# L1 attention's small products moved onto halves of TensorE's rows: 51 rows each, masks first

## The chip, the cores and the metric

One core of one Trainium2 chip runs the whole program in one launch. The metric is device time in microseconds (us), median of the runs shown. The program is a chain of eight layers (four attention-like, four feed-forward) over a residual stream of 2048 tokens by 512 channels; the change touches the third of them, called L1 attention.

## What is computed

The part of the reference that matters here, shortened:

```python
x = x + layernorm(L1_attn(layernorm(x), Wqkv, Wo))

def L1_attn(h, Wqkv, Wo):             # h: 2 batches x 1024 tokens x 512
    qkv = h @ Wqkv                    # 32 query heads of 16, one key and one value head of 16
    q, k, v = split(qkv)
    scores = einsum("bqhd,bkd->bhqk", q, k) * 16 ** -0.5
    scores = scores + alibi           # slope of the head x (key position - query position)
    scores = where(causal, scores, -1e30)
    return (softmax(scores) @ v).reshape(...) @ Wo
```

All heads share one key and one value. The head dimension is only 16, so that a plain score product has 16 rows to contract.

## The kernel before

**Contraction.** Queries and keys are held as pairs of float16 numbers (high part and rest). The rows of `a2_qs` and `a2_ks` stack the parts: four blocks of D2 = 16 rows hold qh, qh, ql, ql against kh, kl, kh, kl (QR = 64), two rows add the ALiBi term (QR to QR+2), and one more row (QR+2) carries minus the row maximum. A maximum product contracts 66 rows, a score product 67. `a2_qs` is [67 rows used, 32 heads, 1024 queries] per batch, `a2_ks[b]` [67 rows, 1024 keys].

**Loops.** Queries go in 16 tiles of 128 (SEQ2: eight of batch 0 in order, then batch 1's as 0, 3, 1, 4, 2, 5, 6, 7). Query tile t attends to t+1 key blocks. For each tile two things are made:

- its *maxima* (`max_unit`): [128 queries x up to 512 keys] for as many heads as fit a PSUM bank, one product a head (L1259), and over the last 128 keys of the diagonal block one identity product with the mask (L1262) for each head; VectorE then reduces the bank to one maximum a head (L1425). Three banks (0 to 2) form this ring.
- its *scores* (`score_unit`): [128 keys x 4 heads x 128 queries] (L1272), on the diagonal block a mask product over all 512 columns (L1275); ScalarE takes the exponential (L1381) out of banks 3 to 5. After four of them `value_units` (L1282) multiplies by the values: four float32 products, which the trace shows as eight, on four column strips of 32 into bank 6.

**Order.** `plan2`, `tails2` and `steps2` write one list, STEPS2, that all engines walk. While tile p's scores are made, tile p+1's maxima are slipped between them, and also the work on the tile before (`heads0` to `lo`: transposes L1323, L1329 and L1342, projection L332 to L334, layer norm). TensorE takes them strictly in that order. A maximum waits until VectorE has emptied its bank (`a2_md`), a score until ScalarE has emptied its own (`a2_e`). A `row` step turns a tile's maxima (L1300) and a DMA (L1197) puts them into row QR+2.

**DMAs.** SyncE copies the key parts (L1189, 4 DMAs a batch) and, for each half batch of 512 queries, the query parts (`q_rows`, L1205): 8 heads x 4 blocks = 32 DMAs. The first maximum of tiles 0 and 4 of a batch waits on `a2_dma` for them.

```python
            for rep, src in enumerate((a2_qh, a2_qh, a2_ql, a2_ql)):
                sp.dma_start(a2_qs[rep * D2:(rep + 1) * D2, h:H2:8, gg * GW:(gg + 1) * GW],
                             src[h * D2:(h + 1) * D2]).then_inc(a2_dma, 16)
```

## Time and profile before

| | us |
|---|---|
| median of 3 runs | 4417.35 |
| lowest, highest | 4415.72, 4435.38 |
| profiled execution, its time | 4429.2 |
| its span in the trace | 4427.4 |
| L1 attention in the trace, first copy of weights to last value product | 660 to 1471 |
| first to last score product | 743 to 1470 |

| engine, whole span | busy us | share |
|---|---|---|
| TensorE products | 3811.0 | 86% |
| VectorE | 2844.1 | 64% |
| ScalarE | 2291.2 | 52% |
| GpSimd | 1786.5 | 40% |

TensorE's busy time counts a product to the end of its pipeline, so products overlap in it; what it can deliver is read from the distance of the starts. "PEclk" is the granted clock as a share of 2.4 GHz; half of it is 1.2 GHz.

### The profile page before, as it was taken

The page shows a single profiled execution, that of the slowest core. Times are in us where ns is not written, and L with a number is a line of the kernel's source. Part 1 is how long each engine was busy: PE and PEld are TensorE (multiplying, and loading weights), DVE is VectorE, ACT ScalarE, POOL GpSimd, SP SyncE. Part 2 cuts the span into 40 slices and gives each one's busy share as a digit, 9 for nine tenths or more (in the row PEclk, how much of TensorE's full clock was granted, in tenths as well). Part 3 has the DMA queues.
Part 4 walks back from the last instruction along what each step waited for, and adds up shares of the span by engine and source line. Part 5 has one row for each costly group of instructions (what it writes and reads, how often), then busy time and mean ns, then how long its engine had stood idle before and what let it go on. Part 6 is the DMA issues. An engine that isn't in the chain of part 4 may idle for free.

```text
span 4427.4 us, 62775 instructions
## 1 busy us (share of the span) xinstructions
PE 3811.0 (86%) x21328; PEld 1913.2 (43%) x21328; DVE 2844.1 (64%) x4571; ACT 2291.2 (52%) x3974; POOL 1786.5 (40%) x1454
## 2 busy tenths in 40 slices
PE   6799995998899648999999999999999966756699
PEld 3344442333333224555555555555555533432344
DVE  6522223674576357888888898888889866566322
ACT  5422222455456436667666676766676644442222
POOL 5400000000000006778787877777787864420000
PEclk9799997889889879999999999999999988897899
DMA  3100001101100010000000000000000010005100
GB/s 108 44 1 0 0 7 35 20 1 21 20 1 1 10 56 12 19 17 7 29 1 24 12 24 13 24 13 13 23 7 23 1 60 1 26 1 137 41 10 19
DMA packets 67429, 97.53 MB, mean 22 GB/s; under 512 B 14081, under 2 KB 39689, under 8 KB 67098
## 3 DMA queue, kind: packets, MB, share of 16 engines
q1 hardware_dynamic: 67100, 93.47, 7.8%
q8 instruction: 166, 2.72, 0.3%
q14 instruction: 163, 1.34, 0.1%
HBM read 77.77 MB, written 6.88 MB: 19 GB/s over the span
## 4 chain that ended last, share of the span: by engine, by line
PE 63%; DVE 15%; issue 8%; ACT 6%; POOL 3%; SPq 3%; DMA 2%; DVEq 0%; POOLq 0%; ACTq 0%
PE psum L332 14%; PE psum L333 13%; PE psum L334 13%; PE psum L1282 3%; PE psum L1259 3%; DVE arena L1425 2%; PE psum L1272 2%; PE psum L2255 2%; PE psum L2243 2%; PE psum L2251 2%; PE psum L2212 2%; SPq L1205 1%; ACT xn L218 1%; PE psum L2234 1%; DVE x L1940 1%
## 5 line engine op out<-in xcount | busy, mean ns | idle before, releaser
L332 PE MATMUL psum<-xt_hi,arena 128*128 128x512 f16 (+1 forms) x2272 | 878.4, 387 | 81.3 <-DVE arena L538 24.3
L333 PE MATMUL psum<-xt_lo,arena 128*128 128x512 f16 (+1 forms) x2272 | 876.3, 386 | 0.0
L334 PE MATMUL psum<-xt_hi,arena 128*128 128x512 f16 (+1 forms) x2272 | 874.7, 385 | 0.0
L2038 POOL TENSOR_TENSOR arena<-arena 128x1024 f16<-128x1024 f16 x256 | 515.3, 2032 | 193.2 <-DVE arena L1850 148.9
L1215 POOL TENSOR_TENSOR rs<-sd,epsc 128x1 f32<-128x1 f32 x16 | 8.8, 548 | 1204.8 <-DVE sd L1469 1204.8
L1425 DVE TENSOR_REDUCE arena<-psum 128x1 f32<-128x512 f32 (+3 forms) x608 | 367.4, 654 | 188.6 <-PE psum L1262 114.7
L332 PE MATMUL psum<-arena 128*128 128x512 f16 (+1 forms) x1152 | 417.7, 367 | 82.1 <-DVE arena L2810 36.3
L1381 ACT ACTIVATE arena<-psum 128x512 f32<-128x512 f32 x576 | 324.4, 598 | 274.9 <-PE psum L1272 181.0
L333 PE MATMUL psum<-arena 128*128 128x512 f16 (+1 forms) x1152 | 417.0, 366 | 0.0
L334 PE MATMUL psum<-arena 128*128 128x512 f16 (+1 forms) x1152 | 416.7, 366 | 0.0
L332 PEld LDWEIGHTS psum<-xt_hi,arena 128*128 128x128 f16 x2272 | 225.5, 99 | 334.9 <-DVE arena L538 27.3
L334 PEld LDWEIGHTS psum<-xt_hi,arena 128*128 128x128 f16 x2272 | 225.6, 99 | 278.9 <-issue 19.0
L333 PEld LDWEIGHTS psum<-xt_lo,arena 128*128 128x128 f16 x2272 | 225.5, 99 | 238.5 <-issue 15.0
L2043 POOL TENSOR_TENSOR arena<-arena 128x512 f16<-128x512 f16 x256 | 316.3, 1254 | 4.2 <-PE psum L2223 4.2
L538 DVE SCALAR_TENSOR_TENSOR arena<-psum,arena 128x512 f32<-128x512 f32 x100 | 69.1, 691 | 355.1 <-PE psum L334 351.5
L1259 PE MATMUL psum<-arena 66*128 66x512 f16 (+3 forms) x768 | 247.3, 362 | 53.9 <-DMA arena<-arena 33.0
L1940 DVE SCALAR_TENSOR_TENSOR x<-arena,x 128x512 f32<-128x512 f32 x288 | 283.5, 985 | 15.4 <-ACT x L1757 8.6
L1940 DVE SCALAR_TENSOR_TENSOR arena<-arena 128x512 f32<-128x512 f32 x288 | 275.3, 956 | 6.8
L2065 POOL TENSOR_TENSOR arena<-arena 128x256 f32<-128x256 f32 x128 | 148.7, 1162 | 250.4 <-ACT arena L1809 250.4
L508 ACT ACTIVATE arena<-psum 128x512 f32<-128x512 f32 x100 | 59.5, 595 | 345.1 <-PE psum L334 345.1
L1272 PE MATMUL psum<-arena 67*128 67x512 f16 x576 | 227.4, 410 | 5.6 <-ACT arena L1381 3.2
L332 PEld LDWEIGHTS psum<-arena 128*128 128x128 f16 x1152 | 124.0, 108 | 195.3 <-DVE arena L2810 36.8
(310 smaller groups left out, 7771.7 us busy)
## 6 DMA issues: line engine op xcount, KB each, us to landing
arena<-m_wi SPq DMA_DIRECT2D x64, 320.0 KB, 2.9
arena<-arena SPq DMA_DIRECT2D x128, 64.0 KB, 2.5
arena<-m_wo SPq DMA_DIRECT2D x32, 256.0 KB, 2.6
arena<-out SPq DMA_DIRECT2D x6, 768.0 KB, 5.9
x<-L_attn_x SPq DMA_DIRECT2D x4, 1024.0 KB, 8.7
out<-x SPq DMA_DIRECT2D x4, 1024.0 KB, 4.3
arena<-gate_wT SPq DMA_DIRECT2D x16, 224.0 KB, 2.5
arena<-up_wT SPq DMA_DIRECT2D x16, 224.0 KB, 2.5
```

The lines of the kernel that those rows point to most:

```text
L332: nc.tensor.matmul(out, lh, rh, start=start, stop=False)
L333: nc.tensor.matmul(out, lh, rl, start=False, stop=False)
L334: return nc.tensor.matmul(out, ll, rh, start=False, stop=stop)
L1259: last = nc.tensor.matmul(out[:, a * w:(a + 1) * w], q, a2_ks[b][0:QR + 2, c:c + w], start=True, stop=not diag)
L1272: last = nc.tensor.matmul(out, a2_ks[b][0:QR + 3, k * P:(k + 1) * P], a2_qs[0:QR + 3, h4 * 4:h4 * 4 + 4, t * P:(t + 1) * P], start=True, s ...
L1282: last = nc.tensor.matmul(psum[j * VW:(j + 1) * VW, 6, :], a2_v[b][:, g % (t + 1), :], a2_ps[(group2[p] + g) % 3][:, j, :], start=False, s ...
L1381: nc.scalar.activation(a2_ps[group % 3][:, u[0] % 4, :], psum[:, 3 + e % 3, :], ACT.Exp).then_inc(a2_e, 1)
L1425: nc.vector.tensor_reduce(a2_mx[:, q % 2, c // 512, h0:h0 + heads], bank[:, 0:heads * w].rearrange("p (h c) -> p h c", h=heads), AXX, ALU. ...
L1940: v = nc.vector.scalar_tensor_tensor(out=out, in0=m4_hb[:, i, j:j + GW], scalar=m4_cp[:, i * KC + j:i * KC + j + 1], in1=out, op0=ALU.mult ...
L2038: nc.gpsimd.tensor_tensor(m4_ar[:, q], heads[q].broadcast_to([P, HG, P]), m4_le.unsqueeze(1).broadcast_to([P, HG, P]), ALU.mult).then_inc( ...
L2043: nc.gpsimd.tensor_tensor(m4_ab[:, q].rearrange("p (h c) -> p h c", c=PS), heads[q].broadcast_to([P, HG, PS]), m4_on[:, 0:PS].unsqueeze(1) ...
L2065: nc.gpsimd.tensor_tensor(m4_sq[:, 0:2, :], m4_sq[:, 0:2, :], m4_sq[:, 2:4, :], ALU.add).then_inc(m4_qs, 1)
```

## The change

The lowest block of products, ql against kl, is dropped: QR = 48, so that a maximum contracts 50 rows and a score 51. The 32 heads are split into two sets of 16, heads with (h div 4) even on partitions 0 to 50, the others on 64 to 114 (`row_group`); the keys stand on both. Products thereby name an array tile of 64 rows x 128 columns at row 0 or 64, where the old ones, and still the masks, named 128 x 128.

`max_units` lists the units of the two sets in turn, and `paired2` gives each maximum of STEPS2 a unit of the set that the last score or maximum before it did not use. The mask of a maximum is now one identity product for all heads of the unit, ahead of their products, which accumulate onto it; the mask of a score still follows it. There are 608 maximum units before and after (352 with a mask), and 576 scores (128 with a mask); mask products of the maxima go from 512 to 352, over the same columns.

```diff
-        QR = 4 * D2
-        a2_qs = carve(0, [H2, TPB * P], F16)
+        QR = 3 * D2
+        HALF = 64
+        a2_qs = carve(0, [H2 // 2, TPB * P], F16)
-        QDMA = 4 + 4 * 8 * 2
+        KDMA, HDMA = 3 * 2, 3 * 8
+        QDMA = KDMA + HDMA * 2
...
-                    units += [(h, 512 // w, first, w) for h in range(0, H2, 512 // w)]
+                    units += [(g * (H2 // 2) + h, 512 // w, first, w) for h in range(0, H2 // 2, 512 // w)
+                              for g in range(2)]
...
+        def row_group(half, first, n):
+            return slice(half * HALF + first, half * HALF + first + n)
...
+        def paired2():
+            left, unit, half = {}, {}, 1
+            for what, p, *u in STEPS2:
+                if what == "score":
+                    half = u[0] % 2
+                elif what == "ring" and RING2[p][0] == "max":
+                    q, n = RING2[p][1:]
+                    rest = left.setdefault(q, list(max_units(SEQ2[q][1])))
+                    other = [m for m in rest if m[2] == rest[0][2] and m[0] // (H2 // 2) != half]
+                    unit[q, n] = other[0] if other else rest[0]
+                    rest.remove(unit[q, n])
+                    half = unit[q, n][0] // (H2 // 2)
+            return unit
...
-                for rep, src in enumerate((a2_qh, a2_qh, a2_ql, a2_ql)):
-                    sp.dma_start(a2_qs[rep * D2:(rep + 1) * D2, h:H2:8, gg * GW:(gg + 1) * GW],
+                for rep, src in enumerate((a2_qh, a2_qh, a2_ql)):
+                    sp.dma_start(a2_qs[row_group(h // 4, rep * D2, D2), h % 4:H2 // 2:4, gg * GW:(gg + 1) * GW],
                                  src[h * D2:(h + 1) * D2]).then_inc(a2_dma, 16)
...
+                h0, heads, c, w = UNIT2[p, u]
+                rows = row_group(h0 // (H2 // 2), 0, QR + 2)
+                diag = c + w == (t + 1) * P
+                if diag:
+                    nc.tensor.matmul(out.rearrange("p (a w) -> p a w", w=512 // heads)[:, :, w - P:w], a2_id,
+                                     a2_mqk.unsqueeze(1).broadcast_to([P, heads, P]), start=True, stop=False,
+                                     skip_group_check=True)
                 for a in range(heads):
...
+                    last = nc.tensor.matmul(out[:, a * w:(a + 1) * w], a2_qs[rows, h0 % (H2 // 2) + a, t * P:(t + 1) * P],
+                                            a2_ks[b][rows, c:c + w], start=not diag, stop=True, skip_group_check=True)
...
+                rows = row_group(h4 % 2, 0, QR + 3)
+                last = nc.tensor.matmul(out, a2_ks[b][rows, k * P:(k + 1) * P],
+                                        a2_qs[rows, h4 // 2 * 4:h4 // 2 * 4 + 4, t * P:(t + 1) * P], start=True,
+                                        stop=(k < t))
```

**TensorE, the maxima of a tile with 384 keys between another's scores.** Before: L1259 is a maximum's product, L1262 its mask, L1272 a score, L1282 the values.

```order
L1259 MATMUL psum<-arena 128x384
L1262 MATMUL psum<-arena 128x128
L1259 MATMUL psum<-arena 128x384
L1262 MATMUL psum<-arena 128x128
L1272 MATMUL psum<-arena 128x512
L1282 MATMUL psum<-arena 32x512 x4
```

After: L1283 is the mask, L1287 the maximum's product, L1298 the score, L1309 the values.

```order
L1283 MATMUL psum<-arena 128x128
L1287 MATMUL psum<-arena 128x384
L1283 MATMUL psum<-arena 128x128
L1287 MATMUL psum<-arena 128x384
L1298 MATMUL psum<-arena 128x512
L1309 MATMUL psum<-arena 32x512 x4
```

The mask stands ahead of its product; each mask names the whole array, its neighbours now half of it.

**TensorE, a unit of four heads with 128 keys, between scores.** Before, a mask behind each head:

```order
L1259 MATMUL psum<-arena 128x128
L1262 MATMUL psum<-arena 128x128
L1259 MATMUL psum<-arena 128x128
L1262 MATMUL psum<-arena 128x128
L1259 MATMUL psum<-arena 128x128
L1262 MATMUL psum<-arena 128x128
L1259 MATMUL psum<-arena 128x128
L1262 MATMUL psum<-arena 128x128
L1272 MATMUL psum<-arena 128x512
```

After, one mask ahead of all four:

```order
L1298 MATMUL psum<-arena 128x512
L1283 MATMUL psum<-arena 128x512
L1287 MATMUL psum<-arena 128x128 x4
L1298 MATMUL psum<-arena 128x512
L1283 MATMUL psum<-arena 128x512
L1287 MATMUL psum<-arena 128x128 x4
```

Four mask products became one of four times the columns.

**SyncE, the first half of batch 0** (key parts, query parts, rows of maxima). Before:

```order
L1180 DMA arena<-mask_qk 128x128
L1181 DMA arena<-mask_kq 128x128
L1189 DMA arena<-arena 16x1024 [waits a2_md]
L1189 DMA arena<-arena 16x1024 x3
L1205 DMA arena<-arena 16x4x512 [waits a2_md]
L1205 DMA arena<-arena 16x4x512 x31
L1197 DMA arena<-arena 1x32x128 [waits a2_e] x3
```

After:

```order
L1203 DMA arena<-mask_qk 128x128
L1204 DMA arena<-mask_kq 128x128
L1213 DMA arena<-arena 16x1024 [waits a2_md]
L1213 DMA arena<-arena 16x1024 x5
L1229 DMA arena<-arena 16x4x512 [waits a2_md]
L1229 DMA arena<-arena 16x4x512 x23
L1221 DMA arena<-arena 2x16x128 [waits a2_e] x3
```

Six key DMAs stand where four were, and 24 query DMAs, of the same size each, where 32 were. Three more small copies (of the ALiBi rows) stand ahead of these.

## Rows read from the trace of the kernel before

**Rows 1.** Engines by stretch: busy us and count of each, PEclk, DMA share, GB/s.

```profile
core 0: us, PE busy (x) PEld busy (x) DVE busy (x) ACT busy (x) POOL busy (x), PEclk, DMA share, GB/s
934.00:1040.00 106.00, 98.39 (x587) 35.68 (x585) 80.87 (x153) 65.54 (x119) 2.19 (x4) 1.00 0.00 1
1086.00:1098.00 12.00, 8.27 (x60) 5.50 (x61) 3.32 (x5) 1.79 (x3) 0.00 (x0) 0.57 0.17 26
1165.00:1190.00 25.00, 21.54 (x66) 6.66 (x67) 11.89 (x21) 7.22 (x13) 0.00 (x0) 0.52 0.08 13
743.00:1470.00 727.00, 662.81 (x3739) 251.79 (x3739) 437.04 (x834) 383.44 (x695) 16.44 (x30) 0.89 0.06 10
```

**Rows 2.** Waits, 743 to 1470: who waited for whom, us, times, longest.

```profile
PEld psum L1259 <- DVE arena L1425: 122.7, 202, 2.4
DVE arena L1425 <- PE psum L1262: 90.8, 73, 16.0
```

**Rows 3.** Groups by line and form, 934 to 1040: count, busy us, mean ns, idle before.

```profile
L1272 PE MATMUL psum<-arena 67*128 67x512 f16 x104 | 39.3, 380 | 0.0
L1259 PE MATMUL psum<-arena 66*128 66x512 f16 x88 | 32.2, 383 | 2.0 <-DVE arena L1425 2.0
L1282 PE MATMUL psum<-arena 128*32 128x512 f32 x208 | 27.7, 605 | 0.0
L1262 PE MATMUL psum<-arena 128*128 128x128 f16 x64 | 14.1, 220 | 0.0
L1272 PEld LDWEIGHTS psum<-arena 67*128 67x128 f16 x104 | 10.1, 98 | 9.8 <-ACT arena L1381 2.0
L1259 PE MATMUL psum<-arena 66*128 66x384 f16 x32 | 10.0, 329 | 1.8 <-DVE arena L1425 1.6
```

**Rows 4.** TensorE in order of time around a group of values: start, us, engine, line.

```profile
1007.83 0.38 PE L1272 MATMUL psum<-arena 67*128 67x512 f16 x1
1008.14 1.06 PE L1282 MATMUL psum<-arena 128*32 128x512 f32 x8
1009.13 0.39 PE L1259 MATMUL psum<-arena 66*128 66x512 f16 x1
1009.36 0.22 PE L1262 MATMUL psum<-arena 128*128 128x128 f16 x1
1009.42 0.38 PE L1272 MATMUL psum<-arena 67*128 67x512 f16 x1
1009.64 0.38 PE L1259 MATMUL psum<-arena 66*128 66x512 f16 x1
```

**Rows 5.** First layers: durations (min/median/max ns) of L1025, then products in order.

```profile
L1025 PE MATMUL psum<-ident,xn x128: 417/421/478, 10.1 to 187.6; 128*128 128x128 f32 x128
...
69.76 1.11 PE L1025 MATMUL psum<-ident,xn 128*128 128x128 f32 x4
70.80 1.86 PE L1052 MATMUL psum<-arena 4*128 4x448 f32 x2
```

**Rows 6.** The same view around a transpose of 32 columns.

```profile
1112.09 0.22 PE L1262 MATMUL psum<-arena 128*128 128x128 f16 x1
1112.15 0.27 PE L1300 MATMUL psum<-ident,arena 128*32 128x128 f32 x1
1112.26 0.38 PE L1272 MATMUL psum<-arena 67*128 67x512 f16 x1
```

**Rows 7.** SyncE in order of time: the copies of key and query parts.

```profile
692.64 2.52 SPq L1189 DMA_DIRECT2D arena<-arena  x4
703.13 21.33 SPq L1205 DMA_DIRECT2D arena<-arena  x32
```

**Rows 8.** TensorE in order of time: its three waits for these copies, in brackets.

```profile
726.49 0.27 PE L1259 MATMUL psum<-arena 66*128 66x128 f16 x1 [22.36 <-DMA arena<-arena]
...
1089.73 0.27 PE L1259 MATMUL psum<-arena 66*128 66x128 f16 x1 [4.82 <-DMA arena<-arena]
...
1168.46 0.58 PE L1259 MATMUL psum<-arena 66*128 66x512 f16 x1 [5.83 <-DMA arena<-arena]
```

More of the change, by code:

```diff
@@ L709, in build @@
         group2 = [first2[p] // 4 for p in range(NT)]
+        def paired2():
[11 more added lines that the diff above has]
+            return unit
+        UNIT2 = paired2()
         s3_raw = carve(0, [KT, C], F32)
@@ L1175, in sp_l1_attn @@
             sp.dma_start(a2_rwo, A["L1_attn_Wo"].rearrange("(k p) n -> p k n", p=P)).then_inc(a2_in, 16)
-            sp.dma_start(a2_qs[QR:QR + 2], A["alibi_q"]).then_inc(a2_in, 16)
-            for b in range(NB):
-                sp.dma_start(a2_ks[b][QR:QR + 3], A["alibi_k"]).then_inc(a2_in, 16)
+            for half in range(2):
+                sp.dma_start(a2_qs[row_group(half, QR, 2)], A["alibi_q"][half]).then_inc(a2_in, 16)
+                for b in range(NB):
+                    sp.dma_start(a2_ks[b][row_group(half, QR, 3)], A["alibi_k"]).then_inc(a2_in, 16)
             sp.dma_start(a2_id, A["ident16"]).then_inc(a2_in, 16)
@@ L1187, in sp_l1_attn @@
                         sp.wait_ge(a2_md, p + 3)
-                        for rep, src in enumerate((a2_kh, a2_kl, a2_kh, a2_kl)):
-                            sp.dma_start(a2_ks[piece[1]][rep * D2:(rep + 1) * D2], src[0:D2]).then_inc(a2_dma, 16)
+                        for rep, src in enumerate((a2_kh, a2_kl, a2_kh)):
+                            for half in range(2):
+                                sp.dma_start(a2_ks[piece[1]][row_group(half, rep * D2, D2)], src[0:D2]).then_inc(a2_dma, 16)
                     elif piece == ("qp", 0, 1, KT - 1):
@@ L1224, in pe_l1_attn @@
             pe.wait_ge(a2_md, 2)
-            pe.wait_ge(a2_in, 16 * 8)
+            pe.wait_ge(a2_in, 16 * 11)
             pe.wait_ge(xt_ok, NT * (s + 1))
@@ L1253, in max_unit @@
                 if u == 0 and t in (0, 4):
-                    pe.wait_ge(a2_dma, 16 * (b * QDMA + (4 + 32 if t == 0 else QDMA)))
-                h0, heads, c, w = max_units(t)[u]
-                for a in range(heads):
-                    q = a2_qs[0:QR + 2, h0 + a, t * P:(t + 1) * P]
-                    diag = c + w == (t + 1) * P
-                    last = nc.tensor.matmul(out[:, a * w:(a + 1) * w], q, a2_ks[b][0:QR + 2, c:c + w], start=True,
-                                            stop=not diag)
-                    if diag:
-                        last = nc.tensor.matmul(out[:, (a + 1) * w - P:(a + 1) * w], a2_id, a2_mqk, start=False,
-                                                stop=True)
+                    pe.wait_ge(a2_dma, 16 * (b * QDMA + (KDMA + HDMA if t == 0 else QDMA)))
+                h0, heads, c, w = UNIT2[p, u]
[5 more added lines that the diff above has]
+                                     skip_group_check=True)
+                for a in range(heads):
+                    last = nc.tensor.matmul(out[:, a * w:(a + 1) * w], a2_qs[rows, h0 % (H2 // 2) + a, t * P:(t + 1) * P],
+                                            a2_ks[b][rows, c:c + w], start=not diag, stop=True, skip_group_check=True)
                 return last
@@ L1271, in score_unit @@
                 out = psum[:, 3 + e % 3, :]
-                last = nc.tensor.matmul(out, a2_ks[b][0:QR + 3, k * P:(k + 1) * P],
-                                        a2_qs[0:QR + 3, h4 * 4:h4 * 4 + 4, t * P:(t + 1) * P], start=True, stop=(k < t))
+                rows = row_group(h4 % 2, 0, QR + 3)
+                last = nc.tensor.matmul(out, a2_ks[b][rows, k * P:(k + 1) * P],
+                                        a2_qs[rows, h4 // 2 * 4:h4 // 2 * 4 + 4, t * P:(t + 1) * P], start=True,
+                                        stop=(k < t))
                 if k == t:
@@ L1347, in act_l1_attn @@
             s = 2 - start
-            act.wait_ge(a2_in, 16 * 8)
+            act.wait_ge(a2_in, 16 * 11)
             nc.scalar.activation(a2_wh, a2_raw, ACT.Copy, scale=WS).then_inc(a2_whi, 1)
@@ L1359, in act_l1_attn @@
                         if b:
-                            act.wait_ge(a2_dma, 16 * (4 + 32))
+                            act.wait_ge(a2_dma, 16 * (KDMA + HDMA))
                         nc.scalar.activation(a2_kh[0:D2, gg * GW:(gg + 1) * GW], bank[0:D2, :], ACT.Copy,
@@ L1422, in dve_l1_attn @@
                         q, unit = piece
-                        h0, heads, c, w = max_units(SEQ2[q][1])[unit]
+                        h0, heads, c, w = UNIT2[q, unit]
                         dve.wait_ge(a2_ms, p + 1)
@@ L2944, in constants @@
     return {
-        "alibi_q": np.ascontiguousarray(np.broadcast_to(np.stack([hi, lo])[:, :, None], (2, 32, 1024))),
+        "alibi_q": np.ascontiguousarray(np.broadcast_to(
+            np.stack([hi, lo]).reshape(2, 4, 2, 4).transpose(2, 0, 1, 3).reshape(2, 2, 16, 1), (2, 2, 16, 1024))),
         "alibi_k": np.stack([pos, pos, np.ones(1024, np.float16)]),
```

4 lines of the change are left out of this document (2 added, 2 removed).

## The prediction

> **What bounds the kernel now.** First the table of stretches [rows 1]. From the first to the last score TensorE's products are in flight for 662.8 of 727 us, VectorE works 437.0 and ScalarE 383.4. Since a product counts to the end of its pipeline, I read what TensorE can deliver from the distance of its starts: two products of 512 columns start 0.22 us apart (1009.42 to 1009.64) [rows 4], a mask of 128 columns takes 0.06 (1009.36 to 1009.42). I take 0.216 for 512 columns. In 934 to 1040, all at 2.4 GHz [rows 1], the groups [rows 3] then need: 104 scores 22.5 us, 88 maxima of 512 columns 19.0, 32 of 384 columns 5.3 (0.165 each), 64 masks 3.7, 26 groups of eight value products at 0.99 (1008.14 to 1009.13) 25.7, and by count and columns about 17 for score masks, projection, keys, transposes and the way into the value products. That is 93 of 106 us, 88%; VectorE needs 80.9, 76%. The waits agree [rows 2]: TensorE's loads for a maximum wait 202 times for VectorE, 0.6 us each, and VectorE waits 73 times for a masked maximum, 1.2 us each. So TensorE is the tighter engine, and VectorE stands close behind. What TensorE gains or loses shows, but not in full; I let 0.85 of it through, between its 88% and all of it less the short waits for VectorE.
>
> **Part 1, half the rows.** Contracting 50 instead of 66 rows is worth nothing by itself: a product of 128 rows (1009.36) [rows 4] and one of 67 stream their columns at the same rate, and columns stay the same. The fewer masks (352 for 512) cover the same columns.
>
> **Part 2, changes of the array's tile.** Before, maxima, scores and masks all name 128 x 128; only the 144 groups of values (and the keys) leave it, 288 changes counted at the values. In the new order I count 554 runs of products on half the rows. Each has a way in and a way out (352 of the ways in come right behind a mask, 244 of the ways out lead to the mask of a maximum, 128 to that of a score, 192 ways touch the values); with 96 changes between values and full products these are 1204, so 916 more. What is one? Around the values [rows 4] a score starts and the values follow 0.31 us later, not 0.22: +0.09. The eight products then hold the array 0.99 us, where 2 rounds of two 512-column passes make 0.86: +0.13, with the starts of four strips in it. The next product is followed after 0.23, +0.01. Together 0.23 for two changes, 0.09 to 0.13 each; I take 0.10. Those are column strips. For rows there is one place [rows 5]: the last of four transposes starts at 69.76 + 1.11 - 0.42 = 70.45, streams four passes of 128 columns (0.21) and should be followed at 70.66; the product of 4 rows comes at 70.80, +0.14. So a change of row tile costs too, and I keep 0.09 to 0.14. Against both stands the transpose of 32 columns [rows 6]: it names another tile, and its neighbours come at 0.06 and 0.11, just their columns. That is the lower end, zero. Half of the changes have the cover of a wait at most (TensorE waits at 202 of 608 maxima); the 352 behind a mask and the 128 ahead of a score's mask have none, since nothing is waited for there.
>
> The sum of this part: 916 x 0.10 = +92 us of TensorE, from 0 to 916 x 0.14 = 128.
>
> The Trainium skill (TensorEngine Tiling (Array Packing), Key Properties) says that changing the tiling mode drains the engine, changing tiles within a mode does not. Rows 4 and 5 agree with it, rows 6 do not show it; by the page this part is the +92, by rows 6 nothing.
>
> **Part 3, opposite halves side by side.** This is the gain. The nearest row for products that share the array is the values [rows 3, 4]: eight of 605 ns, 4.8 us in all, stand in 1.06 us, on four column strips. Two row halves no row shows. If they do the same, neighbours on opposite halves cost one stream. But the planner's alternation is broken by the masks: a masked maximum is put opposite the score *before* it, the mask of the whole array stands between, and the score *after* it is on the same half: 203 runs begin with a maximum and a score of one half. Only 342 pairs of neighbours are opposite. If each product starts as soon as its own half is free, all runs together take 468,736 columns instead of 589,824: 121,088 columns, 51 us. If a following start must also wait for its own weights, 0.098 us to load [rows 3], 71,097 columns remain, 30 us. I take 40 us. The bounds are 0 and 51; a loss has no reason here.
>
> **Part 4, the copies.** 32 query copies take 21.33 us [rows 7], 0.667 each; 24 take 16.0, so 5.3 less. TensorE waits for three of the four bursts [rows 8]: 22.36, 4.82 and 5.83. The first gives 5.3, the next all of 4.8, the last 5.3: -15 us. One burst, the second in order, is not waited for and gives nothing. The two key copies more come when SyncE has nothing to do until 703.13, where it waits for the queries' low parts [rows 7]; nothing. The three more ALiBi copies stand ahead of two masks that the start of the stage needs: 0 to 3 x 0.67 = 2, I take 1. The row copies of the maxima queue behind shorter bursts; no cost. A bonus may come with it: after the two short waits the clock is granted at 0.57 and 0.52 for 12 and 25 us [rows 1]. If the waits go and the clock holds, up to half of 10 and 24 us at 1.2 GHz comes back, 17 us. I count none and keep it in the range.
>
> **The sum.** TensorE: +92 - 40 = +52, of which 0.85 shows: +44. Copies: -15 + 1 = -14. Together +30. Against the profiled execution, 4429.2 (span 4427.4), this makes 4459; that execution was 12 us above the median of 4417.35, and for the median I say 4447.
>
> **Rivals.**
>
> *The changes are hidden.* TensorE waits 122.7 us for VectorE ahead of maxima [rows 2]; if more of the drains fall into these than I let through, say the 244 ways out to a mask and a third of the others, half of the +52 remains, +26, and with the copies' -14 and a few us of clock back the time is 4424, between 4415 and 4437. For it: the load of a maximum waits on 202 of 608. Against it: 480 of the changes stand where nothing is waited for.
>
> *A change of row tile is free, as in rows 6.* This is the one on the other side. TensorE then only gains, 40 us, until VectorE's 76% becomes the bound; from 88% there is room for it, and I let 0.6 through: -24. With -14 and half of the clock's bonus, -8, the time is 4371. It decides against me when a change costs under 0.03 us: 916 x 0.03 = 27 is less than the 40 won. For it speaks one place, against it rows 4 and 5.
>
> *The clock falls.* It is granted at 0.89 over the stage [rows 1], although at 1.00 where TensorE is 88% filled. Were the empty time of the changes to bring it to 0.80, the fifth of the stage at 1.2 GHz would be two fifths: 727 x 0.18 = 131 us more at half rate, half of it lost, +65: 4512. Against it: the order has no longer waits than before.
>
> *No overlap, or no load beneath a product of the same half.* If the halves don't run side by side, 92 x 0.85 - 14 = +64: 4481. If in a run on one half the next load waits for the product, 448 pairs of neighbours on the same half pay 0.098 each [rows 3], +44, of which +37 show: 4484. The Trainium skill (TensorE: Matmul & The Clock Gate, Part 3) does say that weight loads overlap running products only where the row groups differ; by that rule it is the 4484, and the 0.22 us between starts in rows 4, each with a load of its own, does not agree with it.
>
> **How the numbers follow.** Forecast 4447 (4430 to 4470 by its own bounds): 0.44. Hidden, 4424: 0.21. Free changes, 4371: 0.17. Clock, 4512: 0.11. No overlap or no load beneath, about 4482: 0.07. About 0.5%, 22 us, is what a measurement of this kernel can tell from no change, so the borders are 4395 and 4439. Faster: 0.17 of the free changes and 0.01 of the hidden: 0.18. Within: 0.20 of the hidden and 0.13 of the forecast's lower part: 0.33. Slower: the rest, 0.49. The range from 4392 to 4500 leaves out the free changes but their upper end (0.15) and most of half of the clock case (0.05).
>
> **What the changed profile would show.** Right: from a mask to its maximum's product 0.15 us or more where 0.06 stood; a score 0.3 us behind a masked maximum's product only where a mask lies between; opposite neighbours starting 0.01 to 0.1 us apart, not 0.22; 24 query copies in 16 us, TensorE's first wait near 17 us, the short ones gone or under 1; VectorE waiting longer for maxima. The stage, 743 to 1470, should be some 44 - 10 = 34 us longer, the wait ahead of it 5 shorter, and everything after it unchanged. Wrong: masks followed after 0.06 (changes are free), opposite neighbours still 0.22 apart (no overlap), or PEclk in the stage far from 0.89.

## The result, and the profile after

The changed kernel takes 4524.5 us (median of 4 executions, 4496.6 to 4550.5) against 4416.5 for the kernel before beside it: a ratio of 1.0235, 95% interval 1.0165 to 1.0304. It is slower by about 108 us, and beyond the range. The profiled execution took 4531.8 us, its span is 4530.0 (before 4427.4), 102.6 longer.

Where does it sit? From the first to the last score took 726.1 us before and takes 825.8 now (744.7 to 1570.6). TensorE's first product of a maximum (not its mask, which now stands ahead of it) starts 4.7 earlier, and everything behind the last score is 1.5 longer (2959.4 for 2957.9). So the whole loss lies in the stage that was changed. The stretches of the profile of after (from and to, length, busy us and count of each engine, PEclk, DMA share, GB/s) say how; the first is the stage, to be held against the last line of [rows 1], the second is tile 6 of batch 0, from its first score to its last:

```profile
core 0: us, PE busy (x) PEld busy (x) DVE busy (x) ACT busy (x) POOL busy (x), PEclk, DMA share, GB/s
744.00:1570.00 826.00, 768.62 (x3611) 211.65 (x3615) 447.87 (x834) 390.43 (x696) 16.43 (x30) 0.80 0.04 7
1006.00:1090.00 84.00, 79.47 (x312) 17.05 (x311) 43.53 (x75) 36.82 (x65) 1.09 (x2) 0.67 0.00 1
```

The same tile in the kernel before:

```profile
984.00:1040.00 56.00, 52.57 (x310) 18.47 (x307) 41.59 (x75) 35.13 (x64) 1.09 (x2) 1.00 0.00 1
```

Over the stage the granted clock fell from 0.89 to 0.80. In the tile it fell from 1.00 to 0.67: 310 products on TensorE then and 312 now, 75 operations on VectorE both times, in 84 us for 56. VectorE is busy as long as before (437 to 448 us in the stage). The page's row of clocks shows the same over the whole span, a digit for each fortieth. The stage fills the eighth to the fourteenth place; they read 8898898 before, and now 9779777:

```profile
PEclk9799996977977788999999999999999997997899
```

PEclk is a mean of two levels, 1.2 GHz (0.5) and 2.4 GHz (1.0). So it can be turned into time at 1.2 GHz. From the start of the first maximum's product to the start of the last score, which I call the stage from here on, it was 159.4 of 743.0 us before and is 358.8 of 848.7 us after. (The expectations below count it from the first score on, as the fences do: 152.7 before and 335.9 after.)

The waits (who waited for whom, us, times, longest), 744 to 1570, have shifted. The lines answer to [rows 2]: VectorE waited 90.8 us for masked maxima there and 73.0 for those without a mask, together 163.8 for the 233.8 of now; ScalarE waited 181.0 for scores without a mask, now 239.6. TensorE's loads waited 122.7 for VectorE; since a mask now stands ahead of its maximum, two lines of after are their counterpart, 84.6 and 59.1.

```profile
ACT arena L1408 <- PE psum L1298: 239.6, 239, 5.3
DVE arena L1452 <- PE psum L1287: 233.8, 187, 11.1
PEld psum L1287 <- DVE arena L1452: 84.6, 133, 2.5
PEld psum L1283 <- DVE arena L1452: 59.1, 103, 1.2
```

So VectorE and ScalarE wait longer for TensorE, which is the tighter engine now as before, and more so. Its loads wait for VectorE no less than before, but TensorE itself stands empty no longer: it has no product in flight for 57.4 of 826 us (826 less 768.6), where it was 64.2 of 727. Its products in order of time at 2.4 GHz (start, us, engine, line) show both things that the change does, as [rows 4] showed the old spacing:

```profile
816.08 0.39 PE L1287 MATMUL psum<-arena 50*128 50x512 f16 x1
816.30 0.38 PE L1298 MATMUL psum<-arena 51*128 51x512 f16 x1
816.61 0.39 PE L1340 MATMUL psum<-arena 128*128 128x512 f16 x1
...
817.93 0.23 PE L1283 MATMUL psum<-arena 128*128 128x128 f16 x1
818.09 0.39 PE L1287 MATMUL psum<-arena 50*128 50x512 f16 x1
818.32 0.38 PE L1298 MATMUL psum<-arena 51*128 51x512 f16 x1
818.63 0.23 PE L1283 MATMUL psum<-arena 128*128 128x128 f16 x1
...
819.27 0.39 PE L1287 MATMUL psum<-arena 50*128 50x512 f16 x1
819.28 0.39 PE L1298 MATMUL psum<-arena 51*128 51x512 f16 x1
```

A mask (L1283) is followed after 0.16 (817.93 to 818.09) where 0.06 stood, a score by a mask after 0.31 (818.32 to 818.63) where 0.22 would stand: a change of tile costs TensorE 0.09 to 0.10, as forecast. Opposite halves start 0.01 apart (819.27, 819.28): they do run side by side. 218 of the 342 opposite neighbours start less than 0.05 apart. Two products of the same half keep 0.22 (816.08, 816.30), so a load is hidden beneath a product of its own half too. At 1.2 GHz the way in after a mask takes 0.22:

```profile
975.13 0.29 PE L1283 MATMUL psum<-arena 128*128 128x128 f16 x1
975.35 0.50 PE L1287 MATMUL psum<-arena 50*128 50x384 f16 x1
```

The copies came out as said. SyncE's queue and TensorE's first wait, the answers to [rows 7] and [rows 8]:

```profile
692.69 4.17 SPq L1213 DMA_DIRECT2D arena<-arena  x6
703.18 16.16 SPq L1229 DMA_DIRECT2D arena<-arena  x24
```

```profile
721.33 0.58 PE L1283 MATMUL psum<-arena 128*128 128x512 f16 x1 [17.15 <-DMA arena<-arena]
```

24 copies in 16.16 us, a first wait of 17.15 for 22.36, and none of the two short waits is left.

So each local event was as forecast, and the time was not. The question for the experiments is what took the clock, and how much of the loss it is.

### The profile page after: what moved, and what is told of

It is laid out like the page before. It is cut to its first block, busy times and chain, and to the rows that moved or that the text cites. A ratio compares the mean times of both kernels' runs of the same rounds, so it can differ in the third digit from the quotient of the medians.

```text
span 4530.0 us, 62430 instructions
## 1 busy us (share of the span) xinstructions
PE 3925.1 (87%) x21168; PEld 1870.2 (41%) x21168; DVE 2858.2 (63%) x4571; ACT 2296.9 (51%) x3974; POOL 1780.3 (39%) x1454
## 4 chain that ended last, share of the span: by engine, by line
PE 65%; DVE 14%; issue 8%; ACT 6%; POOL 3%; DMA 2%; SPq 2%; DVEq 0%; POOLq 0%; ACTq 0%
PE psum L332 13%; PE psum L333 13%; PE psum L334 13%; PE psum L1309 4%; PE psum L1287 4%; PE psum L1298 2%; PE psum L2282 2%; PE psum L2278 2%; DVE arena L1452 2%; PE psum L2270 2%; PE psum L2239 2%; PE psum L1283 1%; ACT xn L218 1%; PE psum L2261 1%; PE psum L1302 1%
## 5 line engine op out<-in xcount | busy, mean ns | idle before, releaser
L1452 DVE TENSOR_REDUCE arena<-psum 128x1 f32<-128x512 f32 (+3 forms) x608 | 379.4, 657 | 261.8 <-PE psum L1287 257.0
L1408 ACT ACTIVATE arena<-psum 128x512 f32<-128x512 f32 x576 | 329.9, 597 | 360.3 <-PE psum L1298 239.6
L1287 PE MATMUL psum<-arena 50*128 50x512 f16 (+3 forms) x768 | 244.9, 390 | 20.0 <-DVE arena L1452 19.8
L1298 PE MATMUL psum<-arena 51*128 51x512 f16 x576 | 231.4, 456 | 7.8 <-ACT arena L1408 5.4
```

The lines of the kernel that those rows point to most:

```text
L1287: last = nc.tensor.matmul(out[:, a * w:(a + 1) * w], a2_qs[rows, h0 % (H2 // 2) + a, t * P:(t + 1) * P], a2_ks[b][rows, c:c + w], start=no ...
L1298: last = nc.tensor.matmul(out, a2_ks[b][rows, k * P:(k + 1) * P], a2_qs[rows, h4 // 2 * 4:h4 // 2 * 4 + 4, t * P:(t + 1) * P], start=True, ...
L1408: nc.scalar.activation(a2_ps[group % 3][:, u[0] % 4, :], psum[:, 3 + e % 3, :], ACT.Exp).then_inc(a2_e, 1)
L1452: nc.vector.tensor_reduce(a2_mx[:, q % 2, c // 512, h0:h0 + heads], bank[:, 0:heads * w].rearrange("p (h c) -> p h c", h=heads), AXX, ALU. ...
```

## The experiments

All are kernels of the same program. "Changes" counts as the prediction does: how often TensorE goes from a product that names one shape of array tile to one that names another (288 before, 1204 after); the 16 transposes of 32 columns, as in [rows 6], are left out of the count. The stage is that of the profiled execution. The last column takes the price of a us at 1.2 GHz out of it; where the 0.39 comes from stands behind the twelfth kernel. The times at 1.2 GHz are each of one profiled execution. They scatter: ahead of the stage, where no edit changes TensorE's products, it is 114 us before, 190 in e5_padded and 61 in e1_rows51, and yet the first maximum starts within 7 us of the same time in all three. So a difference in that column is leaned on where the stage's length and the median time go with it, and one of a few tens of us is not leaned on by itself.

| kernel | time, us (n) | ratio to before, 95% | changes | stage, us | of it at 1.2 GHz | stage less 0.39 x that |
|---|---|---|---|---|---|---|
| before | 4416.5 (4) | | 288 | 743.0 | 159.4 | 680.8 |
| after | 4524.5 (4) | 1.0235 (1.0165 to 1.0304) | 1204 | 848.7 | 358.8 | 708.8 |
| e1_rows51 | 4759.4 (3) | 1.0774 (1.0752 to 1.0795) | 1681 | 1085.4 | 778.2 | 781.9 |
| e2_nomask | 4441.9 (9) | 1.0048 (1.0026 to 1.0069) | 288 | 760.0 | 306.2 | 640.6 |
| e3_rows51_nomask | 4563.4 (3) | 1.0326 (1.0306 to 1.0346) | 481 | 881.3 | 573.7 | 657.6 |
| e4_halves_nomask | 4440.0 (9) | 1.0050 (1.0031 to 1.0069) | 481 | 744.5 | 304.1 | 625.9 |
| e5_padded | 4398.5 (7) | 0.9956 (0.9937 to 0.9974) | 288 | 719.8 | 123.6 | 671.6 |
| e6_masks_on_halves | 4425.8 (10) | 1.0017 (1.0003 to 1.0032) | 481 | 745.2 | 180.6 | 674.8 |
| e7_mask_changes | 4607.4 (3) | 1.0435 (1.0408 to 1.0463) | 1312 | 928.8 | 477.1 | 742.7 |
| e8_rows128 | 4355.4 (5) | 0.9861 (0.9837 to 0.9885) | 288 | 683.6 | 25.0 | 673.9 |
| e9_halves_rows64 | 4458.8 (4) | 1.0081 (1.0062 to 1.0099) | 1204 | 774.0 | 168.0 | 708.5 |
| e10_masks_rows64 | 4409.7 (8) | 0.9970 (0.9958 to 0.9982) | 481 | 731.7 | 140.2 | 677.0 |
| e11_rows128_changes | 4458.0 (3) | 1.0083 (1.0059 to 1.0107) | 1312 | 783.0 | 116.7 | 737.5 |
| e12_rows128_4blocks | 4377.9 (4) | 0.9903 (0.9887 to 0.9920) | 288 | 698.9 | 43.6 | 681.9 |

Three kernels are over 2% from the before beside them in their whole interval, e1, e3 and e7; the other differences are smaller, but none of the intervals holds 1.

Two theories stood at the start: **changes** of the array's tile cost their own time and leave TensorE's array empty, and **half rows**: products that contract 51 rows for 67 are what loses the clock. A third, that the two halves side by side empty the array between them (**overlap**), was their rival. Ahead of each verdict stands one line, the stretch from the first to the last score of that kernel, with the columns of the first fence.

### Three blocks on one half, no overlap

```diff
-        QR = 4 * D2
+        QR = 3 * D2
...
-                        for rep, src in enumerate((a2_kh, a2_kl, a2_kh, a2_kl)):
+                        for rep, src in enumerate((a2_kh, a2_kl, a2_kh)):
...
-                for rep, src in enumerate((a2_qh, a2_qh, a2_ql, a2_ql)):
+                for rep, src in enumerate((a2_qh, a2_qh, a2_ql)):
```

> The kernel before with the three blocks alone: 50 and 51 rows, all heads at row 0, masks behind the products as before, 24 query copies. Nothing can run side by side; the products name the 64-row tile and the masks the whole array, so the order has 1681 changes of tile (before 288, after 1204). Theory D (each change empties the array and many of them bring the granted clock down): the changed kernel paid about 0.16 us a change, clock included, so 4417 + 1393 x 0.16 - 14 = 4626, PEclk of the stage 0.80 or less. Theory O (the clock falls because overlapped halves leave TensorE empty): clock as before, 0.89, and only the changes' own 0.1 us: 4417 + 1393 x 0.1 x 0.85 - 14 = 4521. Theory R (products on half the rows count less for the clock): clock down to 0.80 or less, time near D's.

```profile
751.00:1805.00 1054.00, 1024.55 (x3738) 272.04 (x3738) 460.21 (x834) 396.48 (x695) 16.43 (x30) 0.65 0.03 5
```

4759 us, slower than either theory allowed. With 51 rows everything on rows 0 to 63 makes 1681 changes, and 778 of 1085 us run at 1.2 GHz. The overlap can't be the cause of the lost clock: here there is none, and the loss is three times that of the change. It does not yet tell changes from half rows.

### The masks left out: of before, of e1_rows51, of after

```diff
-                    if diag:
-                        last = nc.tensor.matmul(out[:, (a + 1) * w - P:(a + 1) * w], a2_id, a2_mqk, start=False,
-                                                stop=True)
...
-                if k == t:
-                    last = nc.tensor.matmul(out, a2_id, a2_mkq.unsqueeze(1).broadcast_to([P, 4, P]), start=False, stop=True)
```

> The kernel before without any mask product (the causal mask is left out, so the output differs): full tiles, 288 changes, no overlap. A baseline for the next two. All theories: the masks' 54 us of columns go, some 45 show: 4370, PEclk of the stage 0.87 to 0.92.

> Three blocks, 51 rows at row 0, no masks (left out): half the rows in every maximum and score, but only 481 changes and no overlap. D: 193 changes more than e2 at 0.1 to 0.16, copies -14: 4372 to 4387, clock as e2. O: clock as e2, 4372. R: clock falls to 0.80 or less though there are few changes: 4440 or more.

> The changed kernel without any mask (left out): both halves, 481 changes, and far more overlap, since no mask stands between: 380,032 columns in sequence where e3 has 589,824, 88 us less. D: the clock holds at 0.87 or more, VectorE becomes the bound, about 40 us under e3: 4340. O: the most overlap of all, so the clock falls most, below 0.80, and the time is over 4400. R: clock falls as in e3.

The stretches of the three, in this order:

```profile
741.00:1486.00 745.00, 676.61 (x3158) 217.23 (x3158) 439.67 (x834) 383.42 (x695) 16.50 (x30) 0.80 0.06 10
```

```profile
735.00:1601.00 866.00, 812.62 (x3158) 228.56 (x3158) 447.61 (x834) 391.17 (x695) 16.43 (x30) 0.68 0.04 6
```

```profile
736.00:1465.00 729.00, 631.26 (x3158) 170.55 (x3158) 435.11 (x834) 377.09 (x695) 16.43 (x30) 0.80 0.05 8
```

The first is the surprise of the study. The kernel before with 640 products fewer, no tile changed and nothing else touched, was expected at 4370 and takes 4442, where the kernel before beside it takes 4417.7: slower than with the masks. Its stage needs 40 us less once the clock is taken out (640.6 for 680.8), and gets it back with interest, because the time at 1.2 GHz goes from 159 to 306 us. Taking work from TensorE can cost time.

The second differs from the first by 51 rows on one half for 67, and by 193 changes: 121 us slower, 574 us at 1.2 GHz. Since e7_mask_changes below loses 318 us to 1024 changes, 193 changes would account for some 60 of the 267 us more at 1.2 GHz (an estimate); the rest is the half rows. The third puts the same products on both halves: 304 us at 1.2 GHz, as many as with 67 rows (306), and the time is that of the first (its profile is of its fastest execution, 4422.0). So the overlap doesn't starve the clock; these half rows side by side hold as much of it as full tiles do. That rival falls. The overlap's worth without the clock is the difference of the last column, 657.6 less 625.9, 31.7 us.

Does the load wait where two products share a half? The second has them in a row, at 1.2 GHz:

```profile
841.25 0.63 PE L1270 MATMUL psum<-arena 51*128 51x512 f16 x1
841.68 0.63 PE L1260 MATMUL psum<-arena 50*128 50x512 f16 x1
842.11 0.63 PE L1270 MATMUL psum<-arena 51*128 51x512 f16 x1
```

They start 0.43 apart, twice the 0.22 of full clock. The load stays hidden.

### The rows filled up to 66 and 67 again

Three blocks of parts, with 16 rows of zeros between them and the ALiBi rows:

```diff
-                sp.dma_start(a2_ks[b][QR:QR + 3], A["alibi_k"]).then_inc(a2_in, 16)
+                sp.dma_start(a2_ks[b][QR - D2:QR + 3], A["alibi_k"]).then_inc(a2_in, 16)
...
+            sp.dma_start(a2_qs[QR - D2:QR + 2], A["alibi_q"]).then_inc(a2_pad, 16)
...
-                for rep, src in enumerate((a2_qh, a2_qh, a2_ql, a2_ql)):
+                for rep, src in enumerate((a2_qh, a2_qh, a2_ql)):
```

> The kernel before with the lowest block of products gone but its 16 rows kept, as zeros: 66 and 67 rows on the whole array as before, 24 query copies instead of 32, no tile changes beyond the 288. Theory R (products that name half of the array's rows bring the granted clock down; e3 against e2: 558 us of the stage at half clock for 291): the clock stays as before, 0.89 in the stage, and only the shorter copies show, 10 to 15 us: 4403 to 4408. If instead the number of rows with data counts (51, as in e3), the clock falls and the time is 4480 or more.

```profile
740.00:1444.00 704.00, 648.22 (x3737) 244.66 (x3737) 435.99 (x834) 383.67 (x696) 16.43 (x30) 0.92 0.05 8
```

4398.5, 21 us faster than the 4419.3 beside it. This is Part 4 of the change by itself: the first maximum 2.2 us earlier, the stage 9.2 shorter without the clock (the two short waits were 10.65) and 36 us less at 1.2 GHz. The last of these is small beside the scatter told above. Against e1_rows51, 16 rows of zeros buy 361 us, but by two things at once: 67 rows are contracted for 51, and they name the tile of 128 rows, so that the 1681 changes are 288 again.

### The masks on the product's own half

The other way to be rid of the changes, in the changed kernel: each mask becomes two products of 64 rows on the half of its neighbours.

```diff
-                    nc.tensor.matmul(out.rearrange("p (a w) -> p a w", w=512 // heads)[:, :, w - P:w], a2_id,
-                                     a2_mqk.unsqueeze(1).broadcast_to([P, heads, P]), start=True, stop=False,
-                                     skip_group_check=True)
+                    own = row_group(h0 // (H2 // 2), 0, HALF)
+                    for j in range(2):
+                        nc.tensor.matmul(out.rearrange("p (a w) -> p a w", w=512 // heads)[:, :, w - P:w],
+                                         a2_id2[own, j], a2_mqk2[own, j].unsqueeze(1).broadcast_to([HALF, heads, P]),
+                                         start=(j == 0), stop=False, skip_group_check=True)
```

> The changed kernel with each mask product split in two that contract 64 rows on the half of their own unit, so that no mask names the whole array: 481 changes of tile instead of 1204, and 616,064 columns in sequence where the changed kernel has 599,808. Theory D (changes, by their emptying and the clock): most of the loss goes, 723 x 0.16 = 116 less: 4410. Theory R (half rows): only the changes' own time goes, 723 x 0.1 x 0.85 = 61 less, and the clock stays low, 0.80: 4460.

```profile
739.00:1467.00 728.00, 652.41 (x4072) 219.59 (x4072) 435.87 (x834) 380.83 (x696) 16.50 (x30) 0.89 0.05 8
```

723 changes fewer and 99 us faster than after, level with before. Its products at 2.4 GHz:

```profile
818.36 0.30 PE L1289 MATMUL psum<-arena 64*128 64x128 f16 x4
818.48 0.39 PE L1293 MATMUL psum<-arena 50*128 50x512 f16 x2
818.70 0.39 PE L1304 MATMUL psum<-arena 51*128 51x512 f16 x2
```

Four masks of 64 rows are followed after 0.12 and a pair of maxima after 0.22, no more than their columns take, so the gap behind a mask is gone. Of the 103.5 us that its stage is shorter than after's, 34 are there without the clock, and 178 us fewer run at 1.2 GHz. So the changes bring both losses. (The edit also makes 960 mask products of 480, over 16,256 columns more in sequence; that this helps the clock a little can't be excluded.)

### Changes alone, in the kernel before

```diff
-                        last = nc.tensor.matmul(out[:, (a + 1) * w - P:(a + 1) * w], a2_id, a2_mqk, start=False,
+                        last = nc.tensor.matmul(out[:, (a + 1) * w - P:(a + 1) * w], a2_id[0:64], a2_mqk[0:64], start=False,
```

> The kernel before, where only the masks of the maxima contract rows 0 to 63 (half of each such mask is left out, the output differs): maxima and scores stay on the whole array, nothing runs side by side, but the order has 1312 changes of tile for 288. It has the changes without the half rows. R: the changes' own time, 1024 x 0.1 x 0.85 = +87, and a small loss of clock: 4504 to 4540, PEclk of the stage 0.83 or more. D: clock and time as in e1, 4700 or more, PEclk 0.70 or less.

```profile
758.00:1655.00 897.00, 856.92 (x3738) 262.56 (x3739) 453.74 (x834) 391.27 (x695) 16.44 (x30) 0.75 0.05 8
```

```profile
1595.76 0.38 PE L1259 MATMUL psum<-arena 66*128 66x512 f16 x1
1596.07 0.23 PE L1262 MATMUL psum<-arena 64*128 64x128 f16 x1
1596.23 0.39 PE L1272 MATMUL psum<-arena 67*128 67x512 f16 x1
```

The plainest test of changes: 512 masks contract 64 rows for 128 (half of each such mask is left out, so that a maximum can also take in keys that come later), maxima and scores are as before, and 1024 changes are added. 188 us slower than the 4419.3 beside it. Every pair of changes shows in the second fence, 0.31 for 0.22 and 0.16 for 0.06. Without the clock the stage is 61.9 us longer, 0.060 for a change; and 318 us more run at 1.2 GHz. The clock is the larger part, by two to one. Not all of it need be the changes': the masks have also lost half of their rows. By e2_nomask, where all masks are gone and no change is added, 147 us more run at 1.2 GHz, so that 318 is more than the missing rows are likely to explain; the two are not separated here.

### All 128 rows

e5_padded with zeros on the rows from 67 on, the row of maxima on row 127, and the products contracting 127 and 128 rows:

```diff
+            nc.gpsimd.memset(a2_qz[64:P], 0.0).then_inc(a2_pz, 1)
...
-                    q = a2_qs[0:QR + 2, h0 + a, t * P:(t + 1) * P]
-                    last = nc.tensor.matmul(out[:, a * w:(a + 1) * w], q, a2_ks[b][0:QR + 2, c:c + w], start=True,
+                    q = a2_qs[0:P - 1, h0 + a, t * P:(t + 1) * P]
+                    last = nc.tensor.matmul(out[:, a * w:(a + 1) * w], q, a2_ks[b][0:P - 1, c:c + w], start=True,
```

> As e5, but the maxima contract 127 rows and the scores 128, zeros in between (the row of the maximum stands on row 127). If the granted clock goes by the rows that a product names, this has the highest share at 2.4 GHz: under 100 us of the stage at half clock where before has 153, so 25 us or more less than e5: 4380 or less. If only the tile (whole array or half) counts: as e5. If rows with data count: as e5, whichever that is.

```profile
731.00:1398.00 667.00, 606.01 (x3733) 233.89 (x3737) 435.18 (x834) 381.75 (x695) 16.49 (x30) 0.98 0.05 8
```

4355.4, faster than both kernels: 64 us less than the 4419.3 of before beside it, by a ratio of 0.9861. The same products in the same order with the same columns, and zeros that add nothing to the sums, leave 25 us at 1.2 GHz. TensorE is empty for no less of the stage than in e5_padded (61.0 of 667 us for 55.8 of 704), so the length of its waits did not bring the clock back. The rows that a product contracts are worth nothing in its own time and a lot in the clock.

### The changed kernel with 63 and 64 rows, and e6_masks_on_halves with them

```diff
-                rows = row_group(h0 // (H2 // 2), 0, QR + 2)
+                rows = row_group(h0 // (H2 // 2), 0, HALF - 1)
...
-                rows = row_group(h4 % 2, 0, QR + 3)
+                rows = row_group(h4 % 2, 0, HALF)
```

Zeros stand between the ALiBi rows and the last row of each half, which holds the maxima.

> The changed kernel, masks and order as they are, but each half contracts 63 and 64 rows instead of 50 and 51, the added rows being zeros. Nothing else changes: 1204 changes of tile, the same overlap. If rows contracted bring clock back (e8 against e5: 20 us of the stage at half clock for 117), the 336 us at half clock fall to 200 to 260 and the time to 4470 to 4500. If in this kernel the clock is lost by the changes of tile alone, it stays within 10 us of 4524.

> e6 (both masks on the half of their unit, 481 changes) with 63 and 64 rows contracted in each half, zeros added. By the rows: half clock in the stage from 163 to under 80 us, at 0.375 us a us 30 less: 4395, perhaps 4385. If rows don't count on halves: 4426 as e6.

```profile
739.00:1490.00 751.00, 692.79 (x3611) 206.17 (x3615) 443.28 (x834) 389.89 (x695) 16.49 (x30) 0.90 0.05 8
```

```profile
735.00:1450.00 715.00, 636.94 (x4072) 218.11 (x4072) 436.13 (x834) 380.51 (x695) 16.44 (x30) 0.91 0.05 8
```

13 rows of zeros on each half give the changed kernel 66 us, with every change of tile still in its place; without the clock its stage is the same, 708.5 for 708.8. That shows both causes: the time at 1.2 GHz in after, 359 us, goes to 168 by the rows alone and to 181 by the changes alone (e6_masks_on_halves). Either is enough to bring most of the clock back, and both together bring little more, 140. I had expected under 80 there (from the first score on it is 130.4); that was missed, and what holds the last 140 is open. The two losses don't add up, and it is their meeting that costs.

### All 128 rows with the changes of e7_mask_changes

```diff
-                        last = nc.tensor.matmul(out[:, (a + 1) * w - P:(a + 1) * w], a2_id, a2_mqk, start=False,
+                        last = nc.tensor.matmul(out[:, (a + 1) * w - P:(a + 1) * w], a2_id[0:64], a2_mqk[0:64], start=False,
```

> e8 (127 and 128 rows) with the masks of the maxima contracting 64 rows only (half of each such mask is left out, the output differs): 1024 changes of tile more at the most favourable number of rows. It asks for a change's own time. If the clock holds (under 60 us of the stage at half clock), all that is added is that time, 0.05 to 0.1 us a change: 4405 to 4455. If changes take clock whatever the rows: over 150 us at half clock and 4470 or more.

```profile
751.00:1502.00 751.00, 711.67 (x3738) 245.07 (x3739) 448.55 (x834) 389.88 (x695) 16.49 (x30) 0.94 0.05 7
```

Beside e8_rows128 this is again 1024 changes, with the 512 masks at 64 rows: +103 us, of them 63.6 without the clock (0.062 for a change) and 92 us more at 1.2 GHz. The change's own time is the same at 67 rows and at 128, and here it hangs less on the price of the clock: with any price between 0.33 and 0.40 it is 0.067 to 0.061, where e7_mask_changes gives 0.079 to 0.057. What the edit takes from the clock is 318 us there and 92 here. The time ended at the upper edge of what was expected, because the clock did not quite hold.

### All 128 rows in the kernel before, with its four blocks

```diff
-                    q = a2_qs[0:QR + 2, h0 + a, t * P:(t + 1) * P]
-                    last = nc.tensor.matmul(out[:, a * w:(a + 1) * w], q, a2_ks[b][0:QR + 2, c:c + w], start=True,
+                    q = a2_qs[0:P - 1, h0 + a, t * P:(t + 1) * P]
+                    last = nc.tensor.matmul(out[:, a * w:(a + 1) * w], q, a2_ks[b][0:P - 1, c:c + w], start=True,
```

> The kernel before with all four blocks and 32 query copies, and only the rows contracted raised to 127 and 128 with zeros. If e8's gain is the clock's: half clock in the stage from 153 to about 20 us, 4417 - 50 = 4367, some 10 to 15 above e8, which has the shorter copies. If e8's gain comes from somewhere else (the start of the stage, the copies), it is near 4400 or above.

```profile
738.00:1421.00 683.00, 611.43 (x3733) 235.79 (x3737) 435.51 (x834) 381.68 (x695) 16.43 (x30) 0.97 0.06 11
```

```profile
999.73 0.39 PE L1268 MATMUL psum<-arena 127*128 127x512 f16 x1
999.95 0.22 PE L1271 MATMUL psum<-arena 128*128 128x128 f16 x1
1000.01 0.38 PE L1281 MATMUL psum<-arena 128*128 128x512 f16 x1
```

Its starts are those of [rows 4], 0.22 and 0.06. Rows alone, with nothing else of the change: 4377.9, a ratio of 0.9903, and 116 us less at 1.2 GHz. It was expected at 4367, a little too low.

**What a us at 1.2 GHz costs.** Four pairs differ by rows alone: before and this one, e5 and e8, after and e9, e6 and e10. Their stages differ by 44.1, 36.2, 74.7 and 13.5 us, their time at 1.2 GHz by 115.8, 98.6, 190.8 and 40.4. That is 0.38, 0.37, 0.39 and 0.33, in all 168.5 / 445.6 = 0.38; e7 and e11, at 145.8 / 360.4 = 0.40, differ by rows and by little else, and with them it is 0.39. A TensorE that alone set the pace would lose 0.5. The figure is for stages like these; in e1_rows51 and e3_rows51_nomask, where most of the time is at 1.2 GHz, it may be higher, and their last column is not used.

## Why the prediction was wrong

The step that failed is the clock, which the sum put at nothing: Part 1 gave half the rows no price at all, and Part 2 priced the changes by their own time alone. The runs showed 199.4 us more at 1.2 GHz in its place, 78 us of time, which comes from the two together: either one taken back (e9_halves_rows64, e6_masks_on_halves) brings most of it back.

The sum of the table's last columns gives the loss of the profiled execution: 199.4 us more at 1.2 GHz x 0.39 = 77.8; the rest of the stage 28.0; the first maximum 4.7 earlier; behind the stage 1.5 later. Together 102.6, the difference of the spans. Against it, step by step:

- **Part 1, half the rows: wrong, the first half of the step that failed.** "Contracting 50 instead of 66 rows is worth nothing by itself", since products of 128 and 67 rows stream at one rate. The rate is the same, but the rows bear on the clock. After with 13 rows of zeros more on each half has 190.8 us less at 1.2 GHz, and takes 66 us less.
- **Part 2, the changes: own price nearly right, effect on the clock left out.** 0.10 on TensorE is what the trace shows (0.16 for 0.06, 0.31 for 0.22), at masks, at scores and at the product that clears the bank of the values (L1340) alike. What shows in time is 0.060 to 0.062 in two pairs of kernels, 60% of it and not 85%: 916 x 0.061 = +56 where 916 x 0.10 x 0.85 = +78 stood. The clock that they take with them has no term in the sum. Taking 723 of them out gives 178 us of 1.2 GHz back; the 34.0 us that this gives besides are 0.047 a change, or 0.057 with the time of the added columns counted.
- **Part 3, the overlap: there, worth half.** The starts are 0.00 to 0.01 apart as said. The rest of the stage, 28.0, and the 10.65 us of short waits that went leave +38.7 for changes and overlap; with +56 for the changes the overlap is -17, where -40 x 0.85 = -34 stood. The -17 is what is left over and was not measured by itself; e3 and e4, where the overlap takes 88 us of columns out and gives 31.7, come to the same share, 18 of 51. The two errors nearly cancel: +38.7 measured for +44 forecast.
- **Part 4, the copies: right.** 16.16 us for 16.0, the first wait 17.15 for 17, the short waits gone, no cost at the start. e5_padded has them alone and is 21 us faster: the -14 and part of the clock's bonus that the prediction named and did not count.
- **The rival "the clock falls": this is what happened.** Its PEclk of 0.80 is the measured one; its mechanism, the empty time of the changes, is half of it, since the rows alone bring as much back. Its chance was 0.11, by the sentence "Against it: the order has no longer waits than before". That sentence is the error of judgement. The clock fell without longer waits: in after, TensorE is busy for 768.6 of 826 us by the page, 93%, more than the 91% before, and has less clock. Its price came out too low as well: 4512 was the sum with 131 us more at half rate, reckoned on the old length of the stage and half of it lost; the trace has 199.4, of which 0.39 is lost.
- **The other rivals.** Changes of a row tile are not free; the transpose of [rows 6] that spoke for it passes free beside full products, and pays among half ones (0.20 ahead of the next score, where 0.11 stood). No stalled load beneath a product of the same half (0.22 and 0.43 apart). Hidden changes: 40% of each is hidden, but with the smaller gain of the overlap +38.7 remains, not this rival's +26.

The Trainium skill (TensorEngine Tiling (Array Packing), Key Properties) says that a change of tiling mode drains the engine; the 0.16 for 0.06 behind a mask agrees with it, and 0.06 us of each shows in the time. It also says (TensorE: Matmul & The Clock Gate, Part 3) that loads overlap running products only where the row groups differ; the 51-row products of one half, 0.22 us apart, each with its own load, do not agree. (The same part also lets a load run ahead when it goes to the background weight buffer; that would fit them, and no run here shows the buffer.)

With the clock's term of +78 the sum of the prediction would have been 4447 + 78 = 4525, within a microsecond of the measured median, in part by luck, since two smaller errors cancel. The bottom line was wrong by that one term. A warning could have been read ahead: [rows 1] has the stage at 0.89, so the clock was already being lost there. That rows bear on it no row of before could show.

What stays open: how the chip comes to its grant. The runs order the kernels (more rows, fewer changes, more products: more clock), and rule out the overlap and longer empty stretches of TensorE as what made it fall. They do not give a rule from which the 140 us of e10_masks_rows64 would follow.

## What to carry to other kernels

Where a stage's granted clock is below 1.0 though its TensorE is busy, price an edit twice: by the engine time that it adds or takes, and by what it does to the clock, since in such a stage fewer rows, a mix of half-array and full-array tiles, or even fewer products can cost more than they save. Filling the contraction up to the full array with rows of zeros is free in the product's own time, and here brought 44 us by itself and 64 with the shorter copies. If products go on half the rows, everything between them should go there too: the overlap of the halves is real, but by the account above it won 17 us, while the changes of tile cost 56 and the clock 78.

## What the runs showed of the hardware

- **Zeros buy clock.** From 66 and 67 to 127 and 128 rows: 159.4 to 43.6 us at 1.2 GHz, and with 24 copies 123.6 to 25.0; the added rows hold only zeros, on both sides. From 50 and 51 to 63 and 64 rows on each half: 358.8 to 168.0.
- **Less work, less clock.** Without the masks 306.2 us at 1.2 GHz for 159.4, and a time 24 us longer.
- **The busy share of TensorE does not foretell its clock.** The kernel e3_rows51_nomask is busy 812.6 of 866 us, 94%, at a clock of 0.68; e8_rows128 606.0 of 667, 91%, at 0.98. Part of it is turned round: a slower clock makes the same products busy for longer. The Trainium skill (TensorE: Matmul & The Clock Gate, Part 1) says that the gate follows how busy the engine has been; the profile's busy column alone does not agree with that here.
- **A tile change costs 0.09 to 0.10 us at 2.4 GHz** whichever way it goes (into a 64-row tile 0.16 for 0.06, out of it 0.31 for 0.22), and 0.06 of it shows in the time here, where VectorE stands close behind.
- **Products on the two halves of the rows can start 0.00 to 0.01 us apart** (819.27 and 819.28; 218 of 342 under 0.05), which no row of before had shown.
